# A sequential scan with work woven into its steps: the order of two blocks of woven work, and an idle stretch before a layer norm

## The reference, cut to what matters

```python
u = x @ W_in + b_in
g = sigmoid(x @ W_gate + b_gate)
def step(h_prev, (u_t, g_t, x_t)):
    h_t = tanh(h_prev @ A + u_t @ Bm)          # 16384 dependent steps
    y_t = h_t @ C.T + u_t @ D.T
    return h_t, g_t * y_t + (1 - g_t) * x_t
ys = scan(step, zeros, ...)
x1 = layernorm(x + (ys @ W_out + b_out + x))
h  = gelu(x1 @ binarize(w1).T + b1)            # 1024 -> 4096
x2 = layernorm(x1 + (h @ binarize(w2).T + b2)) # 4096 -> 1024
```

## Time and profile before

| | us |
|---|---|
| runs: lowest, median, highest of 3 | 12347.74, 12356.65, 12363.4 |
| the profiled execution, own time | 12359.49 |
| its span on core 4, the slowest | 12357.8 |
| spans of the other cores | 12268.1 to 12355.6 |
| granted TensorE clock, mean of a core | 0.533 to 0.539 |

### The profile page before, as it was taken

One profiled execution on the slowest core, in us unless ns is written; L12 is line 12 of the kernel. 1 busy time (PEld: TensorE's weight loads), 2 busy tenths in 40 slices (PEclk: granted clock), 3 DMA queues, 4 the chain that ended last, 5 costly groups with the idle time before them and its releaser, 6 DMA issues.

```text
span 12357.8 us, 229723 instructions; the slowest of 8 cores (12268.1 to 12357.8 us)
## 1 busy us (share of the span) xinstructions
PE 6937.9 (56%) x92416; PEld 4479.9 (36%) x92416; DVE 1076.5 (9%) x1740; ACT 3273.9 (26%) x17002; POOL 402.1 (3%) x529
## 2 busy tenths in 40 slices
PE   0044446764477545764477545764467545764444
PEld 0023333443335333443335333443335333443323
DVE  0110001110020100210020100210020100210021
ACT  0112222222222222222223222322223222222210
POOL 1000000000000000000000000000000000000000
PEclk9855555555555555555555555555555555555566
DMA  4430001330024101230013101230013200230024
GB/s 118 139 87 1 1 1 28 95 93 1 1 50 125 40 1 27 82 106 1 1 38 120 57 1 21 72 108 15 1 34 110 67 1 17 82 103 1 1 59 131
DMA packets 360868, 631.15 MB, mean 51 GB/s; under 512 B 18272, under 2 KB 191840, under 8 KB 357760
## 3 DMA queue, kind: packets, MB, share of 16 engines
q0 software_dynamic: 110464, 280.89, 8.9%
q1 hardware_dynamic: 249344, 335.58, 8.7%
HBM read 618.23 MB, written 46.14 MB: 54 GB/s over the span
## 4 chain that ended last, share of the span: by engine, by line
PE 45%; DMA 17%; ACT 17%; issue 13%; DVE 5%; ACTq 2%; DVEq 0%; POOLq 0%; SPq 0%; POOL 0%
PE pss L905 18%; ACT h_ring L915 16%; PE psd L192 16%; DMA BW<-bw2d 8%; PE pss L909 4%; PE pss L907 3%; PE pss L908 3%; DMA XSL<-xT 2%; DMA BW<-bw1d 2%; DMA F32P<-w 2%; ACTq L914 1%; DMA bw2d<-RBF 1%; PE pst L192 1%; DMA bw1d<-RBF 1%; ACT H2BF L574 1%
## 5 line engine op out<-in xcount | busy, mean ns | idle before, releaser
L915 ACT ACTIVATE h_ring<-pss 128x2 bf16<-128x2 f32 x16384 | 2922.1, 178 | 7966.7 <-PE pss L909 7966.5
L905 PE MATMUL pss<-h_ring,A_bf 128*128 128x1 bf16 x16383 | 3037.3, 185 | 3351.1 <-ACT h_ring L915 3337.5
L905 PEld LDWEIGHTS pss<-h_ring,A_bf 128*128 128x128 bf16 x16383 | 1767.0, 108 | 5408.6 <-ACT h_ring L915 4951.0
L892 PE MATMUL pss<-ub_ring,I_bf 128*128 128x2 bf16 x16384 | 2967.9, 181 | 1.3 <-DVE ub_ring L461 1.3
L907 PE MATMUL pss<-h_ring,A_bf 128*128 128x1 bf16 x16383 | 2732.2, 167 | 0.0
L908 PE MATMUL pss<-h_ring,A_bf 128*128 128x1 bf16 x16383 | 2711.6, 166 | 0.0
L909 PE MATMUL pss<-h_ring,A_bf 128*128 128x1 bf16 x16383 | 2702.9, 165 | 0.0
L892 PEld LDWEIGHTS pss<-ub_ring,I_bf 128*128 128x128 bf16 x16384 | 1866.9, 114 | 222.6 <-DVE ub_ring L461 1.8
L907 PEld LDWEIGHTS pss<-h_ring,A_bf 128*128 128x128 bf16 x16383 | 1913.9, 117 | 0.0
L908 PEld LDWEIGHTS pss<-h_ring,A_bf 128*128 128x128 bf16 x16383 | 1740.5, 106 | 0.0
L909 PEld LDWEIGHTS pss<-h_ring,A_bf 128*128 128x128 bf16 x16383 | 1711.3, 104 | 0.0
(11 more groups left out here) (90 smaller groups left out, 2123.3 us busy)
## 6 DMA issues: line engine op xcount, KB each, us to landing
BW<-bw2d SPq DMA_DIRECT2D x256, 512.0 KB, 4.4
BW<-bw2d POOLq DMA_DIRECT2D x256, 512.0 KB, 3.9
BW<-bw1d POOLq DMA_DIRECT2D x128, 512.0 KB, 4.7
BW<-bw1d SPq DMA_DIRECT2D x128, 512.0 KB, 4.0
XSL<-xT POOLq DMA_DIRECT2D x32, 1024.0 KB, 11.1
F32P<-w1T SPq DMA_DIRECT2D x8, 2048.0 KB, 10.8
F32P<-w2T SPq DMA_DIRECT2D x32, 512.0 KB, 4.0
F32P<-w SPq DMA_DIRECT2D x32, 512.0 KB, 3.5
```

Of the source, the lines that this page charges most:

```text
L892: m0 = eng.matmul(p[:, :], I_bf[:], ub_ring[:, :, slot * G + tl: slot * G + tl + 1], start=True, stop=False)
L905: m1 = eng.matmul(p[:, 0:1], A_bf[:, 0, 0:128], rhs0, start=False, stop=False)
L915: sc_.activation(h_ring[:, :, slot * G + tl: slot * G + tl + 1], p[:, :], AFT.Tanh).then_inc(semh["SS"], 1)
```

## The change

The two planner calls change places, so that in stages 1 to 6 the downstream items come first and the 80 items for the next stage's inputs behind them. And 44 steps without an item are put ahead of layer norm 2.

```diff
@@ plan_downstream
         for th in range(2):
             plan_ffn(s, th, x1_v)
         res2_v = semc["VDS"]
+        pe_pause(44)
         x2_v = plan_layernorm(F32P1, F32P0, None, res2_v)
@@ main loop
     for g_idx in range(NG):
+        if g_idx >= 1:
+            plan_downstream(g_idx - 1)
         if g_idx + 1 < NG:
             ub_ready[g_idx + 1] = plan_uub(g_idx + 1)
-        if g_idx >= 1:
-            plan_downstream(g_idx - 1)
         for tl in range(G):
```

## The result

| | before | after |
|---|---|---|
| median of 8 runs, us | 12352.12 | 12408.78 |
| lowest to highest | 12346.94 to 12364.01 | 12406.36 to 12424.4 |
| ratio, 95% interval | | 1.0046, 1.0036 to 1.0057 |
| profiled execution: span of the slowest core | 12357.8 (core 4) | 12415.4 (core 1) |

The change makes the kernel 56.7 us slower, 0.46%. The forecast was 12403 us, a change of +45 on the 12356.65 of three runs; the 12352.12 here is the median of eight.

A forecast was written before the change was run, and what follows sets the result against it. TensorE's waits for late data, beside the scan's 0.604 us step, were taken to bound the kernel. -90.3 + 99.9 - 65.9 + 96.6 + 6.5 = +46.8, taken as +45, gave 12403 us, range 12370 to 12440.

The forecast's parts named there:

- What bounds the kernel: The scan's step, 0.604 us; an item costs nothing in itself, only waits of TensorE for late data count.
- The count of 848 items and pauses: Weave of a stage before the change: 848 items and pauses in 2048 steps, so 44 more steps fit.
- Part 1: Ahead of layer norm 2: 44 paused steps remove a 12.9 us wait in each of stages 1 to 7, -90.3 us.
- Part 2: Head of stages 1 to 6: first item waits 16.9 us for `XQBF`, loaded behind the `h_ring` copy, +99.9 us.
- Part 3: `XSL` loads, stages 1 to 6: two waits of 7.7 us a stage left, 92.4 in place of 158.3, -65.9 us.
- Part 4: `USTG` behind layer norm 2's VectorE chain: TensorE waits 17.0 us in place of 0.9, stages 1 to 6, +96.6 us.
- Part 5: Feed-forward weights: one more stage whose `BW` load is slowed by the first slab's `XSL` load, +6.5 us.
- B: Rival: VectorE's layer norm 2 chain holds the first slab's load, 38 us more in six stages, about 12441 us; chance 0.08.
- C: Rival: layer norm 2's chain is over when `USTG` is wanted, -50 us in all, 12307 us, faster; chance 0.06.
- D: Rival: parts cancel through shorter `XQBF` wait and feed-forward weight waits of 58; +10 to +20, 12370 to 12380 us; chance 0.14.

The follow-up runs named there:

- experiments 7 to 10: Old order with pauses covering `XSL` too (12082.98 us); then feed-forward weights paced (11465.40); that in the changed order, all covered (11450.73); paced old order, remaining waits covered (11360.99).
- Experiment 1: The kernel before, old order, with only the 44 steps of pause ahead of layer norm 2: 12272.89 us against 12359.69, ratio 0.9927.
- experiment 3: The kernel before, old order, with 12 steps of pause ahead of layer norm 2: 12308.14 us against 12355.94, ratio 0.9960.
- experiment 4: The changed kernel with 34 steps of pause ahead of the downstream items of stages 1 to 7: 12300.79 us against 12359.69, ratio 0.9949.
- Experiment 5: The changed kernel with 32 more steps of pause behind layer norm 2: 12409.55 us against 12359.69, ratio 1.0037.
- experiment 2: The changed kernel without its 44 steps of pause, only the planner calls exchanged: 12513.31 us against 12359.69, ratio 1.0123.
- experiment 9: The kernel with paced feed-forward weights, in the changed order, 34 steps of pause ahead of downstream items, 80 behind layer norm 2: 11450.73 us, ratio 0.9272.

## Why the prediction was right, point by point

The sum was made of waits, and the two traces let each be checked. The table has the slowest core of each, 4 before and 1 after. Both run the bare step at the same pace (below). All in us, stages 1 to 7.

| part | predicted | before | after | difference |
|---|---|---|---|---|
| 1, `YBF` ahead of the sums | -90.3 | 116.9 | 26.7 | -90.2 |
| 2, `XQBF` | +99.9 | 18.4 | 117.3 | +98.9 |
| 3, `XSL` | -65.9 | 158.3 | 100.3 | -58.0 |
| 4, `USTG` | +96.6 | 21.4 | 117.9 | +96.5 |
| 5, `BW` from `bw2d` | +6.5 | 439.2 | 448.9 | +9.7 |
| sum | +46.8 | | | +56.9 |

That the last sum meets the measured 56.7 so closely is in part luck. Waits that the prediction left out add another 6 us (below), and the stages grew by 57. And the table is that of two cores. Averaged over all eight of each profile the five parts are -90.8, +94.4, -41.2, +96.2 and +6.1: the same but for part 3, where core 4 had the highest `XSL` waits of the kernel before. On that average the cores became 85 us longer, about 14 of them because four and not two cores had the slow pace described at the end. So the forecast of +45 is 12 us short for the slowest core, and would be 26 or more short for a typical one. A slip besides: +45 on the 12356.65 of the runs then known is 12401.7, and not 12403.

*What bounds the kernel.* Right, and shown by experiments 7 to 10: steps without an item cost nothing, and the time falls by about the waits that they cover, down to 11361 us. The count of 848 items and pauses is right, 716 + 52 for `plan_downstream` and 80 for `plan_uub`; the description ahead of the prediction, "768 items and 52 pauses", counts the pauses twice.

*Part 1* was right in size and kind. Experiment 1 isolates it (-86.8), experiment 3 shows that it is a stretch of VectorE's work against 0.6 us a step.

*Part 2* was right, 16.0 to 18.5 us in each of the seven stages. Stage 7 of the kernel before was a sample of what stages 1 to 6 became, and experiment 4 takes the wait away by time alone.

*Part 3* was right in kind, the number of waits being 12 as forecast, and is the term that was mis-sized: 8 us too good on the slowest cores, 25 on the average of all. I took 7.7 for each wait. On core 1 the fourth slab's are 7.0 to 7.6, the third slab's 8.6 to 10.2. My reason was that "In the new place no copy of `h_ring` is near". That is so, but other transfers are: the 2 MB load of the next tokens behind the store of the output, and the gate weights behind that, beside which the third slab takes 12.39 us. Which of the two costs how much isn't separated. I had looked at what the loads leave behind and not at what the new place has. Experiment 5 shows the 2 MB load as a neighbour at its worst, with 21.9 us for one slab.

*Part 4*, the wait the diff doesn't show, was derived and not seen, 17.0 us; the trace has 16.8 in stage 1 and 17.1 at the longest. Experiment 5 takes the chain out of its way and the wait is gone, experiment 2 shows that the pause ahead of the sums has no part in it.

*Part 5* fits in sign and size, but I made no experiment on it: the waits for these weights differ by more than that between cores and executions (424 to 449 over the eight cores of the kernel before, 432 to 470 on the slowest cores of the kernels above without pacing), so neither +9.7 nor the average's +6.1 for one more collision is shown. That a collision is there is seen in stage 1 after the change as before, the chain again having one `BW` load of 10.99 us where the slab goes out beside it.

What I left out: the mix's `YBF` (L810) costs 7.2 to 7.7 a stage where it cost 6.1 to 6.7, +6.6 in all (45.1 to 51.7), and about as much on every core. Stage 7 before already showed 7.2 in this order. With the pause at the head of the stage (experiment 4) it is back at 45.0, so it hangs on the late start of the stage; on what exactly was not looked at. The other waits change by 5 us or less either way.

*The rivals.* B, the load held by VectorE, did not happen: the second slab's load went out 14.5 us ahead of the chain's end, landed in 9.6, and no wait for it is left. The operations of that stretch are of L516 to L523, all but one of them with two tensors read, and "SBUF — State Buffer" in the Trainium skill ("Who interferes with whom", the list of which ops grab the shared pair) says that such operations have no two-port mode. So the trace agrees with the page and not with the use that the rival made of it; whether a load issued under a run of casts would be held was not tried. C needed the chain to be over within 9.6 us; it takes 24.6 here. D fell with part 2: every stage has the full `XQBF` wait, and the weight waits did not come down to 58 in stages 1 to 6 (63.4 to 67.7).

## What to carry to other kernels

In this kernel, which weaves work into a dependent chain, what an item costs is only how late its data are. So a moved block is to be priced at both ends: what was hidden behind it and now stands open (here `XQBF`), and what it is queued behind on every engine that it uses, also where the diff doesn't name that engine (here `USTG` behind a layer norm on VectorE). A stage of the kernel before that happens to have the new order is the best evidence there is. And when a pause moves a load in time, look up which large transfers start around its new place: in experiment 5 one 2 MB neighbour took back most of what 32 steps of cover, 19 us, had won (7 us gained in place of 50).

## What the runs showed of the hardware

The bare step, with nothing woven in, has more than one pace, and a core keeps the pace of its execution. Windows over the `h_ring` instructions, 990 us of stage 0: first the kernel before on core 4 and on core 1 (the pairs are the busy time and the count of TensorE's matmuls, of its weight loads and of ScalarE's tanh, of which there is one a step; then come GpSimd, the granted clock, the DMA share and GB/s).

```profile
1000.00:1990.00 990.00, 440.34 (x6553) 306.42 (x6552) 292.19 (x1638) 0.00 (x0) 0.50 0.01 1
...
1000.00:1990.00 990.00, 438.07 (x6592) 303.33 (x6592) 294.28 (x1649) 0.00 (x0) 0.50 0.01 1
```

Then the changed kernel on core 1 and on core 4.

```profile
1000.00:1990.00 990.00, 441.70 (x6554) 307.87 (x6555) 292.27 (x1638) 0.00 (x0) 0.50 0.01 1
...
1000.00:1990.00 990.00, 438.52 (x6588) 303.82 (x6586) 294.19 (x1647) 0.00 (x0) 0.50 0.01 1
```

That is 0.604 us a step or 0.600 to 0.601, at a granted clock of 0.50, the 1.2 GHz level, in all four. Later it is the same: between 4200 and 4700 us of the kernel before, core 4 has 827 tanh and core 1 833. By an estimate from these counts, 990/1638 against 990/1647 makes 54 us over 16384 steps; the slow cores' spans are 72 us above the others' before and 46 to 47 after, on average. Core 4 is among the slow ones in one kernel's profile and among the fast in the other's; core 1 the other way round. The time is that of the slowest core, and where all eight cores kept the fast pace, as in experiment 9's profile (spans 11398.5 to 11419.0), the execution lies some 30 us below the median of its kernel. What sets the pace was not found. It means that a single profile of this kernel can't be compared with another to better than about 50 us, unless the paces are looked at first.
